# Moving a fused linear map in front of the second MLP product, with its eviction on ScalarE and its sum on GpSimd

## The reference, cut to what matters

```python
for i, (shift, mask) in enumerate(zip(SHIFTS, (None, MASK1))):
    x3 = _swin_block(x3, shift, mask, ...)
x3 = x3 @ linw + linb
...
def _swin_block(x, ...):
    ...
    x = sc + x                             # x: after attention
    h = _ln(x, ln2g, ln2b)
    h = jax.nn.gelu(h @ w1 + b1) @ w2 + b2
    return x + h
```

## Time and profile before

| | us |
|---|---|
| median of three runs (3321.54 to 3324.6) | 3324.26 |
| the profiled execution, its own time | 3324.49 |
| its span, first to last instruction | 3323.0 |

### The profile page before, as it was taken

The page is one execution under the profiler, slowest core; times in us unless marked ns, Lnnn a source line. Parts: engine busy times, 40 slices in busy tenths (PEclk is TensorE's granted clock), DMA queues, the critical chain, the costliest instruction groups (busy, mean ns, idle before and its releaser), DMA issues. The chain is left out here.

```text
span 3323.0 us, 104077 instructions
## 1 busy us (share of the span) xinstructions
PE 3126.8 (94%) x40530; PEld 2812.4 (85%) x40530; DVE 2261.1 (68%) x6717; ACT 1674.7 (50%) x4073; POOL 826.2 (25%) x1400
## 2 busy tenths in 40 slices
PE   7996899999999999999999999999999999999689
PEld 6784788888888888888888888888888888888589
DVE  1113677777777777777777778777787777787432
ACT  1111566666666666666655555555555555555221
POOL 4400122222222222222222222222222222222110
PEclk9997899999999999999999999999999999999799
DMA  4421011111111111111211111111111111111285
GB/s 84 121 75 45 20 38 36 38 40 40 38 36 36 36 36 36 37 41 45 49 35 38 24 37 37 34 33 24 37 37 37 31 30 31 37 37 25 54 149 90
DMA packets 246679, 148.39 MB, mean 45 GB/s; under 512 B 31729, under 2 KB 246068, under 8 KB 246586
## 3 DMA queue, kind: packets, MB, share of 16 engines
q1 hardware_dynamic: 244882, 146.95, 19.3%
q0 software_dynamic: 1728, 0.48, 0.1%
HBM read 96.74 MB, written 52.50 MB: 45 GB/s over the span
## 5 line engine op out<-in xcount | busy, mean ns | idle before, releaser
L1455 PE MATMUL rm<-w,ht 128*112 128x160 f32 x4480 | 682.1, 302 | 0.0
L1455 PEld LDWEIGHTS rm<-w,ht 128*112 128x112 f32 x4480 | 610.9, 177 | 5.6
L945 POOL TENSOR_TENSOR rs<-ln_tmp,mhalf 112x4 f32<-112x4 f32 (+1 forms) x128 | 119.1, 930 | 1674.5 <-DVE ln_tmp L1114 1674.5
L1032 ACT ACTIVATE ht<-rm 128x448 f32<-128x448 f32 (+1 forms) x640 | 319.1, 499 | 190.1 <-PE rm L118 190.1
L118 PE MATMUL rm<-z2t_hi,w_hi 128*128 128x448 f32 (+1 forms) x640 | 257.4, 402 | 2.8 <-DVE z2t_rest L1224 1.3
L997 ACT ACTIVATE vb<-ra 113x320 f32<-113x320 f32 x256 | 112.8, 441 | 278.5 <-PE ra L118 276.9
L1342 PE MATMUL ra<-ident,z 112*128 112x112 f32 (+1 forms) x1280 | 163.7, 267 | 68.1 <-POOL z L910 68.1
L118 PE MATMUL rm<-z2t_hi,w_lo 128*128 128x448 f32 (+1 forms) x640 | 218.9, 342 | 0.0
L118 PE MATMUL rm<-z2t_rest,w_rest 98*128 98x448 f32 (+1 forms) x640 | 218.8, 342 | 0.0
L118 PE MATMUL rm<-z2t_lo,w_hi 128*128 128x448 f32 (+1 forms) x640 | 217.9, 340 | 0.0
L910 POOL TENSOR_TENSOR z<-z,one 112x448 f32<-112x448 f32 (+2 forms) x192 | 131.3, 684 | 322.0 <-DVE z L1118 322.0
(11 more groups left out here) (247 smaller groups left out, 9171.8 us busy)
## 6 DMA issues: line engine op xcount, KB each, us to landing
xa<-xs SPq DMA_DIRECT2D x128, 245.0 KB
xr<-xs SPq DMA_DIRECT2D x128, 245.0 KB
xs<-a_tok SPq DMA_DIRECT2D x8, 1960.0 KB, 9.5
xs<-xo SPq DMA_DIRECT2D x64, 245.0 KB
ys<-yz SPq DMA_DIRECT2D x64, 245.0 KB
c_y<-ys SPq DMA_DIRECT2D x48, 260.0 KB
c_y<-ys SPq DMA_DIRECT2D x16, 280.0 KB
c_taps<-in_f_syn SPq DMA_DIRECT2D x24, 126.0 KB, 5.0
```

What stands on the lines that cost most here:

```text
L945: gp.tensor_tensor(rs[1][:, t0:t0 + nt], ln_tmp[1][5][:, t0:t0 + nt], mhalf[:, 0:nt], ALU.pow).then_inc(s_pow, 1)
L1032: act_(ht[:, f * SN + t0 * TT:f * SN + (t0 + nt) * TT], bank_m(i, lm, use)[:, 0:nt * TT], ACT.Gelu_apprx_tanh).then_inc(m_freed(i, lm, use ...
L1455: last = mm(bank_m(i, lm, use)[0:TT, t * DIM:(t + 1) * DIM], ht[:, c:c + TT], keep.w["w2", lm][:, f * DIM:(f + 1) * DIM], start=(f == 0), ...
```

## The change

- TensorE: in layer 1 the L products stand straight behind G9 and ahead of W0. W2 to W5 take the places that they have in layer 0. The ring's list of layer 1 is G0..G9, L0..L3, W0..W5, T2A0, T2C0.
- ScalarE evicts the L products, behind its last gelu and the last part of `fifth_head`, and ahead of the first exponentials: seven activations of 112x160 (a copy scaled by the column `std`), into `xo`, which layer 1 doesn't use otherwise. VectorE's `linear_out` (seven operations) is gone.
- GpSimd adds `xo` to `x1b` in two parts (tiles 0 to 3, 640 columns, and tiles 4 to 6, 480 columns), behind `repeat_rest(z1)`, and raises a new semaphore `s_lin` after each. `base(i, 1)` moves to the end of the body, as in layer 0.
- VectorE waits for the first part at `mlp_out(0)` and for the second at `mlp_out(3)`.
- SyncE's store of a strip waits for W5 in both layers.

```diff
-        MLP_USES = [f"G{g}" for g in range(2 * FT)] + [f"W{n}" for n in range(len(PAIRS))]
+        G_USES, W_USES = [f"G{g}" for g in range(2 * FT)], [f"W{n}" for n in range(len(PAIRS))]
-        RM = [Ring(MLP_USES + T2, 2, {}), Ring(MLP_USES + LIN_USES + T2, 2, {})]
+        RM = [Ring(G_USES + W_USES + T2, 2, {}), Ring(G_USES + LIN_USES + W_USES + T2, 2, {})]
...
# SyncE
-                    sp.wait_ge(*m_freed(i, lm, "W5" if lm == 0 else "L3"))
+                    sp.wait_ge(*m_freed(i, lm, "W5"))
...
# GpSimd
-                if lm == 1:
-                    base(m, 1)
                 if ln is not None:
                     pool.wait_ge(s_norm[0], i + 2)
                     repeat_rest(z1, s_z[0])
+                if lm == 1:
+                    pool.wait_ge(s_x1b, m + 1)
+                    for hf, (t0, nt) in enumerate(HALF):
+                        for n in range(2 * hf, 2 * hf + 2):
+                            pool.wait_ge(*m_freed(i, 1, f"L{n}"))
+                        cols = slice(t0 * DIM, (t0 + nt) * DIM)
+                        gp.tensor_tensor(x1b[:, cols], x1b[:, cols], xo[:, cols], ALU.add).then_inc(s_lin, 1)
...
-                if la == 0:
-                    base(i, 0)
+                if la is not None:
+                    base(i, la)
...
# ScalarE
+                def linear_out(n):
+                    use = f"L{n}"
+                    t0, nt = LPAIRS[n]
+                    act.wait_ge(*m_full(i, 1, use))
+                    if n == 0:
+                        act.wait_ge(s_std, m - NS + 1)
+                        act.wait_ge(s_xo, 32 * NS)
+                        reach(act, s_lin, 2 * (m - NS))
+                    for t in range(nt):
+                        last = act_(xo[:, (t0 + t) * DIM:(t0 + t + 1) * DIM], bank_m(i, 1, use)[0:TT, t * DIM:(t + 1) * DIM],
+                                    ACT.Copy, scale=std[:, t0 + t:t0 + t + 1])
+                    last.then_inc(m_freed(i, 1, use)[0], 1)
...
                     if la is not None:
                         fifth_head(1, i - 1, (1,))
+                    if lm == 1:
+                        for n in range(4):
+                            linear_out(n)
...
# VectorE: linear_out and its four calls are gone, mlp_out(n) of layer 1 stands where layer 0's does
+                    if lm == 1 and t0 in (HALF[0][0], HALF[1][0]):
+                        dve.wait_ge(s_lin, 2 * (m - NS) + 1 + (t0 == HALF[1][0]))
...
# TensorE
+                if lm == 1:
+                    linear(range(4))
                 if lm is not None:
                     mlp_out(0)
...
-                if lm == 1:
-                    mlp_out(2)
...
-                    mlp_out(2 + lm)
+                    mlp_out(2)
...
-                    mlp_out(3 + lm)
+                    mlp_out(3)
...
-                    mlp_out(4 + lm)
+                    mlp_out(4)
...
-                if lm == 0:
+                if lm is not None:
                     mlp_out(5)
-                if lm == 1:
-                    linear(range(4))
```

More of the change, by code:

```diff
@@ L696, in phase_b @@
                                                   sem("o_rec"), sem("o_done"))
-        s_x1b, s_std, s_xm = sem("x1b_done"), sem("std_done"), sem("x_mean")
+        s_x1b, s_std, s_xm, s_lin = sem("x1b_done"), sem("std_done"), sem("x_mean"), sem("linear_added")
         FRONT = ["T1A0", "T1C0", "T1A1", "T1C1", "Q0", "K0", "B0", "V0", "Q1", "V1", "K1", "V2", "V3", "B1"]
@@ L1189, in outputs @@
                                     view(rd, 0, QP, 4, [[HEADS, 2], [0, 3], [0, HD]]), ALU.mult).then_inc(s_od, 1)
[L1191 to L1203, removed]
                 def outputs_lo(j):
@@ L1315, in body @@
                     x1_stats(2, True)
-                if lm == 0:
+                if lm is not None:
                     mlp_out(5)
-                if lm == 1:
-                    for n in range(4):
-                        linear_out(n)
                 if la is not None:
```

## The result

The changed kernel takes 3301.53 us (median of 4 runs, 3296.75 to 3306.61) against 3324.43 us for the kernel before (4 runs, 3321.54 to 3328.63): a ratio of 0.993, 95% interval 0.991 to 0.9951. Forecast were 3291 us and a range of 3273 to 3308. So 23 to 27 us were won where 33 were expected.

What follows compares the result with a forecast made beforehand. TensorE was taken to bound layer 0 and nearly layer 1, with 5% lost there to waits. A strip: 45.81 - 2.08 + 0.94 = 44.67 us, 1.14 saved, 30 times, less end effects: -33.3 us, so 3291; range 3273 to 3308.

Steps and rivals of the forecast that it cites:

- the template: Layer 1's new strip put together from layer 0's: 40.85 + 2.88 + 0.94 = 44.67 us.
- Step (1): Removed waits: `base` leaves the front's normalisation (1.48 us), two bank waits at the linear products' old place go; net -2.08 us.
- step (4): GpSimd's first addition, awaited by VectorE at `mlp_out(0)`: ready 0.5 to 1.3 us early; T1 has 2.7 us to spare.
- (3): TensorE's new bank waits for ScalarE's evictions, ahead of L2 (0.41 us) and W0 (0.53): 0.94 us a strip.
- (5): ScalarE's exponentials after the evictions end by +15.7, TensorE wants them at +17.2: covered by 1.5 us.
- A: Rival: all waits vanish as ScalarE's evictions keep up; up to 62 us won, 3262; chance 0.12 (below 3281).
- B: Rival: ScalarE is slower, eviction pairs at 1.08 us; 10 us saved, 3314; chance 0.13.
- C: Rival: GpSimd's first addition is late, one to one to OT0; 2 us late gives 3350; chance 0.08.
- D: Rival: the 1.4 us wait isn't due to `base` and moves to the next matmul; 10 us slower, 3334; chance 0.05.
- what would show it: Signs listed: 44.7 us strips, no T1 wait for `z`; wrong if VectorE's wait at `mlp_out(0)` names `x1b`.
- likeliest case: The forecast itself, 33.3 us saved to 3291, own range 3281 to 3302; chance 0.62.

Runs made afterwards that it cites:

- turn_in_gap: Changed kernel, group 2's scores between L1 and L2 and evicted before W0, turn T1 between L3 and W0, `base` split: strip 43.54 us, 3254.94 us, ratio 0.9787.
- base_last: Kernel before with only `base(i, 1)` moved to the end of the body: strip 45.50 us, 3312.97 us, ratio 0.996.
- late_add: Changed kernel with one more GpSimd operation of 640 columns ahead of the two additions: strip 45.28 us, 3307.53 us, ratio 0.9947.
- vector_evicts: Changed kernel with the linear products evicted by VectorE, not ScalarE, GpSimd's additions kept: strip 47.76 us, 3377.84 us, ratio 1.0171.

## Why the prediction was right, and where it wasn't

**The sum.** Its terms, for a strip:

| term | forecast | measured |
|---|---|---|
| strip before | 45.81 | 45.86 |
| layer 0's strip | 40.85 | 40.85 |
| 28 linear matmuls | 2.88 | 2.81 |
| bank waits ahead of L2 and W0 | 0.41 + 0.53 | 0.53 + 0.54 |
| W0 to T1, longer than in layer 0 | 0 | 0.08 |
| OT0 to the next G0, longer than in layer 0 | 0 | 0.13 |
| strip after | 44.67 | 44.95 |
| saved | 1.14 | 0.91 |

The first row's 0.05 is a slip in the earlier trace rows: the window of layer 1 was closed at 2465.16, and G0 starts at 2465.22. The price of one eviction was good, 0.40 us forecast and 0.393 measured. L2's wait is 0.12 longer than forecast because the matmuls ahead of it are done sooner (+10.70 and not +10.78) and the bank is free 0.04 later; linear products and waits together are 3.88 where 3.82 stood. W0's matmuls last 2.97 and not 2.88 when TensorE comes out of a wait (in the earlier trace rows and in turn_in_gap, without a wait, 2.88). The term that was mis-sized is the template: "I put layer 1's new strip together from layer 0's" took all 2.08 us of difference as waits. Of them 0.12 stays with the new order: from the product Q0 to the attention outputs of group 1 it is 1.07 us in layer 1 before (2440.30 to 2441.37) and after (2434.77 to 2435.84), and 0.95 in layer 0 (1009.82 to 1010.77). Layer 0 before, then layer 1 after:

```profile
1009.82 0.46 PE L118 MATMUL ra<-z1t_hi,qkv_hi 128*128 128x400 f32 x1
...
1010.77 0.66 PE L1422 MATMUL so<-vb,pt 49*49 49x33 f32 x40
```

```profile
2434.77 0.46 PE L118 MATMUL ra<-z1t_hi,qkv_hi 128*128 128x400 f32 x1
...
2435.84 0.66 PE L1426 MATMUL so<-vb,pt 49*49 49x33 f32 x40
```

The outputs wait there for VectorE's biased scores, which start 0.85 us behind the scores in layer 1 and 0.75 in layer 0. Layer 1 looks up its table of biases by the strip; that this is the cause is argued, not shown.

**Step (1) had the wrong cause.** "`base` leaves the place beside the front's normalisation, so its 1.48 us go" is refuted by both runs: alone the move wins 0.36 us, and undone in the changed kernel it costs nothing. In its place: `base` takes 4.7 to 5.2 us of GpSimd's chain to `z1` wherever it stands, `z1` comes some 13.6 to 13.9 us behind G0, and only the linear products ahead of T1 (wanted at +12.55 without, +16.5 with them) cover that. The sum came out near all the same, since step (4) worked out both times and found 2.7 us to spare (measured 2.97). As advice the step would have misled: it promises 44 us for moving `base` alone, and base_last won 0.36 x 30 = 11.

**Steps (3), (4), (5).** (3) held to 0.13 us. (4) held: GpSimd's chain ended its first addition at +15.06 where +14.7 to +15.5 stood, inside the slack forecast. Of the subtraction for group 0 it said that `base` could hold it up at no cost: it took 1.09 us and not 0.67, up to `base`'s end and 0.5 more, and the normalisation still waited 1.66 us for `inv_std`. (5) held: no wait for an exponential showed in the steady strips.

**The rivals.** A and B were sized by an eviction other than the nearest row's and didn't come. C didn't come; late_add shows its slope, 0.33 us for 0.4, which the prediction had as one to one. D said that the gap could merely move; for `base` alone that is nearly what happens, the gap stays at 1.07 of 1.42 us. One sentence under what would show it was too strong: VectorE's wait does name `x1b` in 9 strips, and yet GpSimd was 1.15 us early.

**Chances and range.** The outcome, faster by more than 0.2%, had been given 0.89, and 3301.5 lies in the range, at the late end of the likeliest case's 3281 to 3302. The terms add up to 44.94 where 44.95 was measured, closer than the 0.04 us by which layer 0's own strip differs between executions.

## What to carry to other kernels

When two layers run the same loop and one has gaps, the other is a template for the strip without them, but check at each handover that the two are alike there, since a difference in an address or an operand stays. A gap has two cures, a shorter chain or more work ahead of the waiter; before one is given the credit, work out when the late thing comes and when it is wanted in both. Moving a filler on the first engine wins nothing if the next engine's chain starts no earlier, so reorder both queues together: TensorE's alone lost 0.14 us a strip, both won 0.75.

## What the runs showed of the hardware

A wait of 1.67 us of TensorE ahead of W0 in every strip, in vector_evicts, went with a granted clock of 0.63 in the 4.6 us that followed, and cost 1.67 us on top of the wait. In the kernel before, waits of 1.42, 0.45 and 0.38 us in a strip left the clock at 1.00 in all of layer 1. These waits differ in place as well as in length, and no run tells which of the two counts. What the pair does show is that a wait can cost more than its own length, so the granted clock behind it is to be read as well.

Coming out of a wait at full clock cost 0.09 us over 20 matmuls (2.97 and 2.88 us). A normalisation of VectorE that began beside a running GpSimd operation stood until that one had ended (2.62 us for the first of seven operations, 0.35 for each other), while VectorE's eviction of W0 in late_add, with one input in PSUM, took its usual 0.49 us beside GpSimd's second addition.
